# A new order of units, projections and maxima in the four attentions with 16-wide heads

## The reference, cut to what matters

```python
# 16 heads, 16 wide; s = 1024
Q, K, V = split_heads(x @ Wq.T), split_heads(x @ Wk.T), split_heads(x @ Wv.T)
scores = jnp.einsum('bhqd,bhkd->bhqk', Q, K) / jnp.sqrt(16.0)
scores = jnp.where(jnp.tril(jnp.ones((s, s), bool)), scores, -jnp.inf)
attn = jax.nn.softmax(scores, axis=-1)
out = jnp.einsum('bhqk,bhkd->bhqd', attn, V)
return out.transpose(0, 2, 1, 3).reshape(b, s, 256) @ Wo.T
```

## Time and profile before

| | us |
|---|---|
| median of three runs | 3059.16 |
| the profiled execution | 3057.11 |
| its span | 3055.4 |
| PE busy in the span | 2915.5 (95%) |
| DVE busy | 1355.9 (44%) |
| ACT busy | 1153.7 (38%) |

### The profile page before, as it was taken

How to read it: one execution, slowest core, us unless ns; L and a number is a source line. 1 busy time by engine, 2 the same in 40 slices (tenths; PEclk the granted TensorE clock), 3 DMA queues, 4 the chain that set the end, 5 groups by cost and what they waited for, 6 DMA issues and landing times. The chain is left out here.

```text
span 3055.4 us, 40214 instructions
## 1 busy us (share of the span) xinstructions
PE 2915.5 (95%) x14953; PEld 1770.7 (58%) x14969; DVE 1355.9 (44%) x3179; ACT 1153.7 (38%) x2113; POOL 576.9 (19%) x729
## 2 busy tenths in 40 slices
PE   7989999999999999999999999999999999999978
PEld 4453455644465556556666666656676677654545
DVE  7758425686134114311333333333333332268588
ACT  3645514546132113111443334333344343225576
POOL 2021002130012222222000000012333332130165
PEclk9999999999999999999999999999999999999989
DMA  3021000030102232333100000000000010111031
GB/s 98 17 63 50 25 25 27 4 83 2 51 12 86 85 91 60 85 95 86 38 16 12 11 11 11 18 32 11 11 16 17 11 39 13 39 47 40 12 102 59
DMA packets 70509, 122.98 MB, mean 40 GB/s; under 512 B 15918, under 2 KB 45968, under 8 KB 70048
## 3 DMA queue, kind: packets, MB, share of 16 engines
q1 hardware_dynamic: 68716, 119.09, 13.0%
q10 hardware_dynamic: 1600, 1.31, 0.3%
HBM read 93.26 MB, written 1.54 MB: 31 GB/s over the span
## 5 line engine op out<-in xcount | busy, mean ns | idle before, releaser
L222 POOL TENSOR_TENSOR scale<-scale,powers 128x1 f32<-128x1 f32 (+1 forms) x98 | 57.5, 586 | 1405.0 <-DVE scale L203 1405.0
L2450 DVE TENSOR_TENSOR L1f_inner<-psum,L1f_gate 128x512 f32<-128x512 f32 x96 | 66.3, 691 | 350.8 <-PE psum L2347 350.6
L1654 ACT ACTIVATE L2b_tanh<-psum,L2b_inverse 128x512 f32<-128x512 f32 x192 | 110.6, 579 | 269.7 <-PE psum L1602 268.3
L2431 ACT ACTIVATE L1f_gate<-psum 128x512 f32<-128x512 f32 x96 | 57.1, 597 | 388.0 <-PE psum L2325 388.0
L1232 ACT ACTIVATE L0f_weights<-psum 128x1024 f32<-128x1024 f32 (+1 forms) x192 | 148.9, 812 | 108.7 <-PE psum L1056 81.9
L2304 POOL TENSOR_TENSOR L1f_inner<-L1f_inner,L1f_weight 128x512 f32<-128x512 f32 x96 | 119.3, 1265 | 354.4 <-DMA L1f_weight<-combine 340.3
L1611 PEld LDWEIGHTS psum<-L2b_v,L2b_weights 128*128 128x128 f32 x1152 | 139.6, 191 | 40.2 <-issue 28.7
L2091 ACT ACTIVATE L2a_probs<-psum,L2a_negmax 128x512 f32<-128x512 f32 (+7 forms) x128 | 95.0, 742 | 172.3 <-DVE L2a_negmax L2125 172.2
L1602 PE MATMUL psum<-L2b_q,L2b_k 128*128 128x512 f32 (+3 forms) x384 | 149.8, 487 | 1.0 <-DVE L2b_q L1720 0.8
L1611 PE MATMUL psum<-L2b_v,L2b_weights 128*128 128x129 f32 x1152 | 143.6, 276 | 5.8 <-POOL L2b_weights L1520 5.8
L1978 PE MATMUL psum<-L2a_k,L2a_q 128*128 128x512 f32 (+3 forms) x384 | 145.1, 487 | 0.0
(11 more groups left out here) (536 smaller groups left out, 6104.8 us busy)
## 6 DMA issues: line engine op xcount, KB each, us to landing
L1f_w<-in_L1f_w SPq DMA_DIRECT2D x32, 384.0 KB, 3.6
L1f_weight<-combine SPq DMA_DIRECT2D x32, 384.0 KB, 4.4
L1f_weight<-combine SPq DMA_DIRECT2D x32, 256.0 KB, 4.5
scan_spread_b<-bc SPq DMA_DIRECT2D x16, 512.0 KB, 3.7
L0f_qs<-L0f_part SPq DMA_DIRECT2D x96, 64.0 KB, 2.6
experts_early<-in_L1f_w SPq DMA_DIRECT2D x16, 384.0 KB, 3.6
L2a_early<-in_L2a_w SPq DMA_DIRECT2D x16, 384.0 KB, 3.0
L2b_early<-in_L2b_w SPq DMA_DIRECT2D x16, 384.0 KB, 3.0
```

Of the source, the lines that this page charges most:

```text
L1654: nc.scalar.activation(tanhs[u % 3][:, at:], ps_scores[u % 3][:, at:], ACT.Tanh, scale=inverse[e][:, NT + kt:NT + kt + 1]).then_inc(capped, 1)
```

## The change

The order of units becomes: three units of half 0, the four of half 1, and the last of half 0. The projections are reordered with them, p2 and p3 being now (2, 0) and (3, 0), and p4 and p5 (0, 1) and (1, 1). v0 moves ahead of p2. The pieces after m20 are no longer spread unit by unit: the steepest of the remaining demands sets the rate until it is met, then the next. t is appended to its slot's list at the end. The transposes r2 and r3, and y4, y6, f0 move with the units: r3 needs quad 3 of half 1, which is now unit 6.

```diff
-QUAD_UNITS = [(0, 0), (1, 0), (0, 1), (1, 1), (2, 1), (3, 1), (2, 0), (3, 0)]
-PROJECTIONS = [(0, 0), (1, 0), (0, 1), (1, 1), (2, 0), (3, 0), (2, 1), (3, 1)]
+QUAD_UNITS = [(0, 0), (1, 0), (2, 0), (0, 1), (1, 1), (2, 1), (3, 1), (3, 0)]
+PROJECTIONS = [(n, half) for half in range(2) for n in range(4)]
...
-    order = ("p0 p1 p2 p3 v0 p4 m0 m1 m2 p5 m3 m4 m5 p6 m6 m7 m8 v1 m9 m10 p7 m11 v2 m12 m13 t0 "
+    order = ("p0 p1 v0 p2 p3 p4 m0 m1 m2 p5 m3 m4 m5 p6 m6 m7 m8 v1 m9 m10 p7 m11 v2 m12 m13 t0 "
...
-    at_slot = {}
+    at_slot = {f: [] for f in range(2 * len(KEY_TILES))}
+    todo = [m for m in pieces if m not in order]
+    until = {u: sum(m in todo for m in pieces[:FIRST_PIECE[u + 1]]) for u in range(2, len(QUAD_UNITS))}
+    done = slot = 0
+    while done < len(todo):
+        u = max((u for u in until if until[u] > done), key=lambda u: (until[u] - done) / (due[u] - 2 - slot))
+        for n in range(done, until[u]):
+            at_slot[slot + (n - done) * (due[u] - 2 - slot) // (until[u] - done)].append(todo[n])
+        done, slot = until[u], due[u] - 2
     for u in range(1, len(QUAD_UNITS)):
-        todo = [m for m in pieces[FIRST_PIECE[u]:FIRST_PIECE[u + 1]] if m not in order]
-        a, b = max(due[u - 1] - 2, 0), due[u] - 2
-        for n, m in enumerate(todo):
-            at_slot.setdefault(a + n * (b - a) // len(todo), []).append(m)
-        at_slot.setdefault(due[u], []).append(f"t{u}")
+        at_slot[due[u]].append(f"t{u}")
...
-    then(4, 1, "r2")
-    then(6, 1, "r3")
-    if factor:
-        then(7, 0, "f0")
-    else:
-        then(7, 0, "y4")
-        then(7, 1, "y6")
+    then(5, 1, "r2")
+    then(7, 1, "r3")
...
-        return order + ["z0", f"a{k - 1}", f"a{k}", "b0", f"n{u}", "b1", "r1", "w0"]
-    return order + ["z0", "z1", f"a{k - 1}", f"a{k}", "z2", "z3", f"n{u}", "r1", "w0", "w1", "w2", "w3"]
+        return order + ["z0", "f0", f"a{k - 1}", f"a{k}", "b0", f"n{u}", "b1", "r1", "w0"]
+    return order + ["z0", "z1", "y4", f"a{k - 1}", f"a{k}", "y6", "z2", "z3", f"n{u}", "r1", "w0", "w1", "w2", "w3"]
...
             for u in range(NU):
-                if u < 2:
-                    stack(u, 1)
-                elif u < QUADS:
-                    stack(u, 1)
-                    stack(u, 0)
+                if u + 2 < NU:
+                    stack(*QUAD_UNITS[u + 2])
                 place_max(u)
...
-                if r >= EARLY:
-                    pe.wait_ge(rests, projections.index((n - 2, half)) + 1)
+                if n >= 2:
+                    before = projections.index((n - 2, half))
+                    pe.wait_ge(rests if before < EARLY else firsts, before + 1)
...
-                if g < 2:
-                    pe.wait_ge(firsts, EARLY + 2 * g + 2)
+                if g == 0:
+                    pe.wait_ge(rests, EARLY)
+                elif g == 1:
+                    pe.wait_ge(firsts, len(PROJECTIONS))
...
                 taken(dve, f"m{FIRST_PIECE[u + 1] - 1}")
+                if u >= 2:
+                    taken(dve, f"t{u - 2}")
```

## The result

The changed kernel takes 3074.3 us (median; 3073.4 to 3074.7), 1.0044 times the kernel before (95% interval 1.0029 to 1.0059). The ratio is an estimate from the single executions, not the quotient of the two medians, which is 1.0049. A fifth execution took 6033.7 us in a slow state and is left out. The forecast was 3066, with a range of 3050 to 3073: the sign is right, the size is not, and the measured time lies above the range. The profiled execution has a span of 3072.4 us, 17.0 more than before, where the steps had summed to 6.8.

What follows compares the result with a forecast made beforehand. DVE was taken to bound s0 to s11, PE s75 to s83, both nearly full between. Terms 4 x 0.7 + 3.6 + 1.8 - 1.3 - 0.1 = +6.8 us gave 3063.9 profiled, 3066 as median; range 3050 to 3073.

Steps and rivals of the forecast that it cites:

- First stretch: s0 to s18 with 39 pieces, against old s0 to s10 plus s75 to s82: -1.0 us a stage (-2.6 to +0.7).
- Late turn: t behind the a pair makes PE wait for the DMA at half-1 units: +1.2 us a stage (-0.6 to +3).
- s83 to s87: Last slots before s88, now of a half-1 unit, 5.0 us where 4.77 before: +0.2 us (0 to +0.6).
- r0: This transpose falls into s19 to s23, where DVE is full; its copy is 0.69 us: +0.3 us (0 to 0.7).
- Both are close to full: In the 16-slot stretches between s11 and s75, PE and DVE were both held nearly full (23.96 us for the first).
- End of L0a: After s88, y6's spread stands ahead of n7's division in DVE's queue, delaying w0: +1.8 us.
- End of L3a: After s88, same mechanism and price as in L0a: y6's spread delays n7's division and w0, +1.8 us.
- Ends of L0f: After s88 of both L0f, f0 goes behind z0, so r1 comes later: +0.9 us each (0.3 to 1.5).
- Starts: Before s0: first L0f -1.3 us (0 to -3) by filling m0's wait; L0a and second L0f 0; L3a -0.1.
- A: Rival: the spreading pays, DVE never idle in s0 to s18, PE catches up: -8.7 us, about 3050; chance 0.17.
- B: Rival: a wash, the middle -0.5 us a stage with ends as forecast: +2 us, 3061; chance 0.36.
- C: Rival: the late turn costs in full, 4.2 us a stage in place of 1.2: 3078 us; chance 0.06.

Runs made afterwards that it cites:

- the old head: The changed kernel with p0 p1 p2 p3 v0 at the head of the list again, as before the change: 3072.4 us, 1.0043.
- the 8 matmuls of the delay: The kernel before with 8 matmuls on zeros added ahead of L0a's p0, nothing else: 3062.0 us, 1.0014.
- 16 matmuls: The kernel before with 16 matmuls on zeros added ahead of L0a's p0, nothing else: 3062.4 us, 1.0013.

## Why the prediction was right in sign and short in size

The time came out 8.3 us above the forecast and 1.3 above the end of the range.

- **First stretch: the step that failed.** "-1.0" was +0.9 in each stage, beyond the step's own upper end of +0.7: 7.7 us of the 10.2 that the span came out above the sum. Two sizes were off. DVE's work is 26.5 us, not 25.5: 19 slots also hold n0's division (0.25 + 0.42), which the sum left out; the other 0.35 is not assigned. And DVE is idle 2.5 us rather than 1.65, 0.74 of it ahead of t2's copy, a wait that the late turn brings into this stretch and that the forecast had put at nothing. That the stretch is bound by DVE stands: busy 91%, before 92%. These are readings of the profile; no experiment changes this stretch alone, and turns first everywhere made it longer, through the clock.
- **Late turn: right, and the largest single loss.** Chain 2.81 for 3.0, wait 1.07 for 1.5, and yet 0.44 to 0.46 lost in L0a at each of units 4, 5 and 6 (0.45, 0.45, 0.3 forecast). That the shorter wait cost as much may be DVE's idle time ahead of the copy, 0.50 us each time; this is not shown by itself. Undoing it from unit 4 on gave 1.5 us a middle. The Trainium skill's page "DMA: Bandwidth & Descriptors" (the table of a transfer's cost) has ~2.0 us fixed; this DMA landed 2.29 after its issue began, so the row was nearer. What no step had is that the same edit returned another 6 us outside the middles, where 13 us less at the low clock account for them.
- **s83 to s87**: -0.04 for +0.2. **r0** lengthens s19 to s23 by 0.7 us, but s19 to s34 by 0.1 only (24.08, before 23.96), for +0.3. "Both are close to full" was too much said of these 16 slots, where DVE was busy 19.71 of 23.96 us.
- **End of L0a**: +1.8 to w0, by the mechanism named, and the same in every profile with this end. The fall of the clock behind it went unforeseen, though a wait of 3.22 us for ACT that the kernel before has there shrank to 2.52 and took in part of it. **End of L3a**: 3.4 for 1.8. Seven profiles have this end: 1.8 us in the two without a fall in the first 50 us behind s88, 2.4 to 2.7 in the three with one, 3.3 and 3.4 in the two with two. So the forecast's 1.8 is the term without falls, and the clock adds the rest. **Ends of L0f**: r1 is 0.45 later, half of the 0.9; that the table's 1.6 meets the forecast's 1.7 is luck.
- **Starts**: the first L0f's -1.3 was +0.1 and L0a's 0 was +1.4. The sum named v0's move and priced it at 0 in L0a; it is 0.8 in each. m0's wait halved to 1.64 us as said, but PE then waited 1.17 us for DVE a little later, and the clock fell there in place of behind m0's. The one profile without that fall has -2.4. The Trainium skill's page "TensorE: Matmul & The Clock Gate" (Part 1) lets activity release the clock; the fall behind the waits of 1.64 and 1.17 us agrees, and the forecast took for granted the activity that DVE then held up. The second L0f's 0 was about +0.5 (from the first matmul of its p0 to s0 36.5 us, before 36.0). L3a's -0.1 was 0.0, and there v0's move pays: without it the start is about 2 us longer, a wait that the sum didn't name.
- **Rivals.** A is out (s0 to s88 grew in all four). B's middle of -0.5 is out. C's 3078 is nearer to 3074.3 than the forecast, but by luck: its chain of 3.3 us was 2.8, its waits of 1.8 were 1.1, and its price of 4.2 us a stage for the late turn was about 1.5.

Open: how the clock's falls spread over single executions, and what the spreading is worth by itself. Per-edit prices under 2 us for the whole kernel rest on one profiled execution each. Those of the middles repeat to 0.2 us over the kernels that share the list, stage by stage; L3a's middle is up to 0.8 us longer than the others with the new order (123.44 against 122.55 to 122.70), which is not explained.

## What to carry to other kernels

Where one engine bounds a stretch, count every instruction it has there, also the ones of other work that the longer stretch now spans, and let its idle time grow with the length of the stretch. A chain of transpose, copy and DMA needs its full length (2.8 us here) ahead of its user where PE is the bound. Put early into a stretch that another engine bounds, it makes PE wait for that engine sooner instead (4.2 against 2.5 us here). A microsecond of waiting on PE can cost twice, once by itself and once by a fall behind it, so compare mean granted clocks before reading a difference of a few microseconds as the edit's. And a repair that helps one stage is to be read in every stage that shares the list: the old head gave 0.8 us back twice and lost about 2 in L3a.

## What the runs showed of the hardware that was not expected

Of one kernel, time follows the mean granted clock almost one to one: with the 8 matmuls of the delay 3057.6 us at 0.993 and 3073.2 at 0.988 (0.005 of 3060 is 15 us). Between kernels it need not: the kernel before and the changed one are 17.0 us apart at the same 0.992.

At the program's start PE runs at half pace, and the clock column doesn't show it. PE's timeline with the 8 matmuls and the projections behind them, the window over the 8, and the timeline with 16:

```profile
15.79 3.57 PE L332 MATMUL psum<-zeros 128*128 128x512 bf16 x8 [0.98 <-PEq L102]
19.15 7.89 PE L998 MATMUL psum<-hT,L0a_early 128*128 128x512 f32 x16
```
```profile
15.80:19.10 3.30, 3.30 (x8) 1.34 (x9) 0.00 (x0) 0.00 (x0) 2.07 (x2) 1.00 0.00 0
```
```profile
15.83 6.39 PE L332 MATMUL psum<-zeros 128*128 128x512 bf16 x16 [0.98 <-PEq L102]
22.06 7.03 PE L998 MATMUL psum<-hT,L0a_early 128*128 128x512 f32 x16
```

The 8 start 0.42 us apart on average (3.36 us to the next row); behind L0a nine of them take 2.11 in all, 0.23 each. PE had come out of waits of 9.04 and 1.66 us. The 1.00 in the window is no measurement: the trace's records of the granted clock begin only at 20.9 us in this execution (21.5 with 16 matmuls), and where there is no record the view counts the clock as full. The pace changes where the records begin: the projections' matmuls start 0.85 us apart up to 20.86 us and 0.43 apart from 21.30 on. With 16 matmuls ahead all 16 of the projections' run at the full pace, 7.03 us in place of 7.89. That is part of why the delays came out as 2.8 and 4.6 us at s0. A clock read before a trace's first record says nothing.
